# A fifth product of a tile with B goes from VectorE to GpSimd, and the w1/w2 ring gets three places

## The chip, the cores and the metric

The kernel runs on one core of one Trainium2 chip. The metric is the device time of one execution in microseconds (us); less is better. The core has TensorE (PE), VectorE (DVE), ScalarE (ACT), GpSimd (POOL) and SyncE (SP), each with its own queue of instructions in order, and they wait for each other on semaphores.

## The reference

All data are float32. The input is x of 4 sequences of 2048 positions and 256 features. First a Mamba block with a residual, then a gated feed-forward block with a residual, each closed by a LayerNorm:

```
xz = x @ in_proj.T;  xc, z = halves (512 channels each)
u = silu(causal_conv(xc, 4 taps) + bias)
dt_lo, B, C = split(u @ x_proj.T)            # 64, 16, 16
delta = softplus(dt_lo @ dt_proj.T + dt_b);  A = -exp(A_log)
for t:  h = exp(delta_t * A) * h + (delta_t * u_t) * B_t;  y_t = sum_n h * C_t
x = layernorm(x + ((y + u*D) * silu(z)) @ out_proj.T)
g = silu((x @ w1.T)*s1) * ((x @ w2.T)*s2)    # 1024 wide
g = gelu((g @ h1.T)*s_h1);  g = gelu((g @ h2.T)*s_h2)
x = layernorm(x + (g @ w3.T)*s3)
```

The state h has 512 channels x 16 state numbers per sequence.

## The kernel before

There are two stages. The first (`mamba_stage`) goes over 16 tiles of 512 positions, four per sequence: the whole Mamba block, the LayerNorm and the products with w1 and w2, whose results are stored. The second does the wide layers h1, h2 and w3 on TensorE. The change lies in the first stage alone.

A tile's scans. The 512 channels are taken in four chunks c of 128. A chunk has four steps q of four state numbers each, so a tile has 16 steps k = 4c + q. A step has four groups j, each 128 partitions (32 channels x 4 state numbers) by 512 positions. So a tile has 64 groups. For a group ScalarE computes the decay into a PSUM bank (`decay_of`, L916), and VectorE runs one scan (L1284) over decay and db into h.

db, the product (delta*u)*B of a step, is one instruction of 128x2048. For q = 0, 1, 2 it is VectorE's (`times_b`, L1268): TensorE spreads B's rows over the partitions into PSUM (`spread_b`, L632), and VectorE multiplies by du_bc. For q = 3 (QV) it is GpSimd's (`times_b`, L1155), which can't read PSUM: once a tile ScalarE copies the spread rows into b_row in SBUF (`rows_sb`, L865), the same rows for all four chunks. GpSimd also has the products of h with C (`times_c`, L1144), two pieces of 128x1024 a step, and two small products of softplus per chunk (L1163, L1167). TensorE sums these over the state numbers (`fold_step`, L659).

The order is written out by hand. Every engine runs through 64 slots i of a tile; n = i + 20 is the group that VectorE scans in the slot (n from 64 on is the next tile). In a slot with n = 4m GpSimd does, in this order: the first piece of C of step m-1, the product with B of step m+1 if it is its own, and the second piece of step m-1. VectorE does the scan of group n and then its product of step m+1. Softplus of the next tile's chunk 0 has slots 21 to 27, on GpSimd 26 and 27 (n = 46, 47).

Rings. db has two places (DBSTEPS): the product of step k waits until the scans of step k-2 are done, and the first scan of step k waits for the product. h has three places, the last step of a tile takes that of the step two before it; hc has two. There are three banks for decays, which run two slots ahead.

w1 and w2 come in eight chunks m of 256 KB through a ring of W12RING = 4 buffers. `copy_product` on ScalarE issues the load of chunk m + 4 behind the second product of chunk m (products e = 2m, 2m+1, slots AB_PLACES), the last four being the next tile's. For the last tile's products a closing pass (`closing`) runs all 16 in a row.

The LayerNorm of the tile (L952, slot 15), its transposes on TensorE (L687, slots 16 to 21), and the x_proj results (L851, L852, slot 18) lie near the new copy's slot. p_dt is a PSUM bank that the softplus steps and the first transpose share.

Of the kernel before, what the change touches and what calls it, by code (L numbers as in the profile page):

```python
# [36 lines left out]

QV = QN - 1
EPS = 1e-5
EXP_LN = "natural_log_exp_and_others"  # L40
# [58 lines left out]
ROWS_SLOTS = (42, 44, 46, 50, 54)  # L99
ROWS = len(ROWS_SLOTS)  # L100
X_SLOTS = (47, 48, 49, 49, 51, 52, 53, 53)

# [16 lines left out]
AB = len(AB_PLACES)  # L119
ABRING, W12RING = 3, 4  # L120
W12_SLOTS = (2, 30)
# [74 lines left out]
def mamba_stage(nc, sems, flag, xT, x, in_wT, conv_w, conv_b, xp_wT, dt_wT, dt_b, A_log, D_param, out_wT,  # L196
                fold, spread, ident, w1T, w2T, h1T, h2T, w3T, scales, d_rows, du_rows, w12, x1, ab):
    ctx = ExitStack()
    with ctx:
# [38 lines left out]
        x_t = [sb(f"x_t{i}", [P, KM, NT], F32R) for i in range(2)]  # L238
        w12_sb = [sb(f"w12_{i}", [P, 2, KM, P], F32R) for i in range(W12RING)]
        ab_sbuf = [sb(f"ab{i}", [P, NT]) for i in range(ABRING)]  # L240
        res = sb("res", [P, SUB, DM])
# [70 lines left out]

        b_bc = sem("b_bc")
        decay = sem("decay")
        db_dve, db_pool = sem("db_dve"), sem("db_pool")
# [85 lines left out]
        def _(sp):  # L401
# [21 lines left out]
            def copies(t, c):  # L423

                k = c % 2
                sp.wait_ge(delta, t.count(KI, c + 1))
                sp.dma_start(d_rows[k], sp_r[k][:]).then_inc(d_out[k], 16)
                sp.wait_ge(du, t.count(KI, c + 1))
                sp.dma_start(du_rows[k], sp_w[k][:]).then_inc(du_out[k], 16)

                sp.wait_ge(db_dve, t.count(KI * QV, QV * (c - 1) + DVE0))
                sp.sem_inc(waited, 1)
                sp.wait_ge(db_pool, t.count(KI, c - 1 + POOL0))
                sp.sem_inc(waited, 1)
                sp.wait_ge(du_out[k], t.count(32, 16 * (c // 2 + 1)))
                for nn in range(GN):
                    sp.dma_start(du_bc[k][nn * GD:(nn + 1) * GD, :, :],
                                 du_rows[k].rearrange("(j d) t -> d j t", d=GD)).then_inc(du_in[k], 16)

                sp.wait_ge(decay, t.count(NG, GC * (c - 1) + DECAY0))  # L440
                sp.sem_inc(waited, 1)
                sp.wait_ge(d_out[k], t.count(32, 16 * (c // 2 + 1)))
                for nn in range(GN):
                    sp.dma_start(d_bc[k][nn * GD:(nn + 1) * GD, :, :],
                                 d_rows[k].rearrange("(j d) t -> d j t", d=GD)).then_inc(d_in[k], 16)
# [67 lines left out]
            def closing(t):  # L513
                for m in range(KH):
                    if m == 2:

                        sp.wait_ge(decay, t.count(NG, 3 * GC + DECAY0))
                        sp.wait_ge(db_dve, t.count(KI * QV, 3 * QV + DVE0))
                        sp.wait_ge(db_pool, t.count(KI, 3 + POOL0))
                    elif m == 6:  # L520
                        sp.wait_ge(h1_round, H1_PIECES)
                    sp.dma_start(first_abr[m][:], ab[1, 2 * m:2 * m + 2].rearrange("e p t -> p e t"))\
                      .then_inc(first_in[m // (KH // 2)], 16)
# [16 lines left out]
        def _(pe):  # L540
# [98 lines left out]
            def spread_b(t, k):  # L639
                c, q = divmod(k, QN)  # L640
                if k == 0:
                    pe.wait_ge(xd_lo, t.count(1, 1))

                pe.wait_ge(db_dve, t.count(KI * QV, QV * c + q + DVE0))
                spread_rows(p_b, t, q, b_bc)
# [45 lines left out]
            def transposed(t, k, step):  # L691
                dst = bank[XT_PLACES[k][1]]
                if step == 0:
                    if k == 0:
                        pe.wait_ge(ln_out, t.count(SUB, SUB))
                        pe.wait_ge(sp_dve, t.count(2 * KI, 2 * KI) if exists(t) else t.count(2 * KI, 0))
                    elif exists(t.following()):
# [8 lines left out]
            def ffn_product(t, e):  # L706
# [5 lines left out]
                if which == 0:  # L712
                    pe.wait_ge(w12_in[m % W12RING], t.count(16 * KH // W12RING, 16 * (m // W12RING + 1)))
                before = product_before(t, e)
# [65 lines left out]
            def tile(t):  # L780
                nxt = t.following()
                for i in range(NG):
# [5 lines left out]
                    if n % JC == 1:  # L788
                        now, g = at_group(t, n - 1 + 2 * JC)
                        if exists(now) and g // JC % QN < QV:  # L790
                            spread_b(now, g // JC)
# [7 lines left out]
                    for part in OUT_SLOTS.get(i, ()):  # L799
                        if exists(t):  # L800
                            project(t, *part)
                    if exists(t):
                        ffn(t, i)
                    if t is LAST_ROW[-1] and i == FIRST_SLOT:
# [11 lines left out]
        def _(act):  # L816
# [8 lines left out]
            def front(t, i):  # L825
# [28 lines left out]
                elif i - 1 in ROWS_SLOTS:  # L854
                    r = ROWS_SLOTS.index(i - 1)
                    act.wait_ge(rows_mm, t.count(ROWS, r + 1))
                    if r == 1:

                        act.wait_ge(db_pool, t.count(KI, POOL0))
                        dst = b_row[:]  # L860
# [128 lines left out]
            def copy_product(t, e):  # L989
# [8 lines left out]
                elif e % 2 == 1 and exists(t):  # L998
                    load_w12(t.following(), m - KH)

# [81 lines left out]
            def tile(t):  # L1082
                nxt = t.following()
                for i in range(NG):
# [26 lines left out]
                    if exists(nxt.following()):  # L1111
                        early(nxt.following(), i)
                    if exists(t):
                        ffn(t, i)
                    if t is LAST_ROW[-1]:
# [12 lines left out]
        def _(pool):  # L1128
# [19 lines left out]
            def times_b(t, k):  # L1148

                c = k // QN  # L1150
                pool.wait_ge(du_in[c % 2], t.count(2 * COPIES, COPIES * (c // 2 + 1)))
                if c == 0:
                    pool.wait_ge(rows_sb, t.count(ROWS, 2))
                pool.wait_ge(scanned, t.count(NG, JC * (k - DBSTEPS + 1) + SCANNED0))
                pool.tensor_tensor(db[:, k % DBSTEPS], du_bc[c % 2][:],  # L1155
                                   b_row[:].unsqueeze(1).broadcast_to([P, JC, NT]), ALU.mult).then_inc(db_pool, 1)

# [30 lines left out]
            def tile(t):  # L1188
                nxt = t.following()
                for i in range(NG):  # L1190
# [4 lines left out]
                    if n % JC == 0:  # L1195
# [3 lines left out]
                        now, g = at_group(t, n + JC)  # L1199
                        if exists(now) and g // JC % QN == QV:  # L1200
                            times_b(now, g // JC)
# [9 lines left out]
            def round_piece(j):  # L1211

                if j == 0:

                    pool.wait_ge(first_lo, KH)
                    pool.wait_ge(db_dve, LAST_ROW[-1].count(KI * QV, KI * QV + DVE0))
                    pool.wait_ge(folded, LAST_ROW[-1].count(NK, NK + FOLDED0))
# [24 lines left out]
        def _(dve):  # L1242
# [19 lines left out]
            def times_b(t, k):  # L1262
                c, q = divmod(k, QN)
                dve.wait_ge(b_bc, t.count(KI * QV, QV * c + q + 1))
                if q == 0:
# [5 lines left out]
            def scan(t, g):  # L1271
# [3 lines left out]
                if j == 0:  # L1275
                    if q < QV:
                        dve.wait_ge(db_dve, t.count(KI * QV, QV * c + q + 1 + DVE0))
                    else:
                        dve.wait_ge(db_pool, t.count(KI, c + 1 + POOL0))
                    dve.wait_ge(saved, t.count(NK, holder_before(H_SLOT, k) + 1 + SAVED0))  # L1280
# [43 lines left out]
            def closing(t, i):  # L1324
# [6 lines left out]
                elif i == GATE_SLOT + 3:  # L1331
                    for m in range(KH):
                        dve.wait_ge(first_hi, m + 1)
                        if m == 0:

                            dve.wait_ge(decay, t.count(NG, NG + DECAY0))
                            dve.wait_ge(db_pool, t.count(KI, KI + POOL0))
                        dve.tensor_tensor(first_parts[1][:, m, :], first_abr[m][:, 1, :],
# [9 lines left out]
            def tile(t):  # L1348
                nxt = t.following()
                for i in range(NG):  # L1350
# [10 lines left out]
                    if n % JC == 0:  # L1361
                        now, g = at_group(t, n + JC)
                        if exists(now) and g // JC % QN < QV:
                            times_b(now, g // JC)
# [740 lines left out]
```

## Time and profile before

| what | us |
|---|---|
| median of 3 runs | 3012.06 |
| lowest, highest | 3010.54, 3012.91 |
| the profiled execution | 3011.42 |
| its span in the profile | 3009.6 |
| busy in the span: PE, DVE, ACT, POOL | 2720.0, 2297.7, 2033.7, 1704.2 |

The busy times are over both stages. In the profile's slices GpSimd is at 8 or 9 tenths up to slice 24 of 40 and at nothing later, VectorE at 9 up to slice 25 and at 4 later. A timeline merges instructions of a kind that follow each other; x5 is five of them, and the time is that from the first's start to the last's end.

### The profile page before, as it was taken

The numbers are of one execution on the slowest core, as the hardware profiler recorded it, in microseconds if no ns is written. First come the engines' busy times: TensorE is split into PE (matmuls) and PEld (weight loads), VectorE is DVE, ScalarE is ACT, GpSimd is POOL, SyncE is SP. The second block draws the span as 40 slices with busy tenths as digits, with TensorE's granted clock in tenths as the row PEclk, the third lists the DMA queues.
The fourth block names the chain that finished last, engine by engine and source line by source line (L and its number), as shares of the span: only waits on it lengthen the run. The fifth ranks groups of instructions, "written<-read, shape, count | busy, mean of one in ns | idle before, by whom it ended". The sixth has DMA issues, their size and how long they took to land. (4 is left out here: it accounts for less than half of the span.)

```text
span 3009.6 us, 40984 instructions
## 1 busy us (share of the span) xinstructions
PE 2720.0 (90%) x11540; PEld 1619.3 (54%) x11540; DVE 2297.7 (76%) x2650; ACT 2033.7 (68%) x3600; POOL 1704.2 (57%) x839
## 2 busy tenths in 40 slices
PE   5798998998998998998998976999999999999997
PEld 2243443343443443443443432778888888888886
DVE  6999999999999999999999999144445444444452
ACT  3878877878878877877878877465544555555452
POOL 4899999999899989999999998100000000000000
PEclk8899999998999999999999987999999999999999
DMA  8565565565566565565565566632222222222210
GB/s 265 122 188 158 144 190 158 144 193 164 134 193 165 136 192 159 139 196 158 139 192 165 143 186 224 205 101 77 92 70 70 84 91 77 70 79 88 70 42 15
DMA packets 239646, 412.05 MB, mean 137 GB/s; under 512 B 23264, under 2 KB 63456, under 8 KB 239456
## 3 DMA queue, kind: packets, MB, share of 16 engines
q1 hardware_dynamic: 175680, 297.67, 36.6%
q10 hardware_dynamic: 63776, 112.22, 11.4%
q8 instruction: 73, 1.20, 0.2%
q14 instruction: 117, 0.96, 0.1%
HBM read 285.55 MB, written 124.26 MB: 136 GB/s over the span
## 5 line engine op out<-in xcount | busy, mean ns | idle before, releaser
L1284 DVE TENSOR_TENSOR_SCAN h<-bank,state,db 128x512 f32<-128x512 f32 x1024 | 1243.3, 1268 | 18.9 <-ACT bank L916 18.5
L1144 POOL TENSOR_TENSOR hc<-h,c_rows 128x1024 f32<-128x1024 f32 x512 | 1200.3, 2375 | 96.6 <-DVE h L1284 75.0
L916 ACT ACTIVATE bank<-d_bc,a_neg 128x512 f32<-128x512 f32 x1024 | 695.4, 685 | 251.8 <-DVE h L1284 240.6
L1625 ACT ACTIVATE hring<-s_bank,sc 128x512 f32<-128x512 f32 x248 | 170.4, 687 | 488.6 <-PE s_bank L1558 488.3
L1558 PE MATMUL s_bank<-mid,h_r 128*128 128x512 f32 x2048 | 468.7, 390 | 4.6 <-DVEq L1652 4.6
L1268 DVE TENSOR_TENSOR db<-bank,du_bc 128x2048 f32<-128x2048 f32 x192 | 435.7, 2269 | 2.5 <-issue 2.5
L1558 PEld LDWEIGHTS s_bank<-mid,h_r 128*128 128x128 f32 x2048 | 385.5, 188 | 85.6 <-ACTq L1596 5.0
L731 PE MATMUL bank<-x_t,w 128*128 128x512 f32 x1088 | 362.5, 461 | 60.7 <-ACT ab L993 53.9
L659 PE MATMUL bank<-hc,fold_w 128*32 128x512 f32 x2048 | 305.1, 671 | 23.0 <-DVE uz L1308 11.3
L731 PEld LDWEIGHTS bank<-x_t,w 128*128 128x128 f32 x1088 | 203.2, 200 | 216.6 <-ACT ab L993 101.0
L1155 POOL TENSOR_TENSOR db<-du_bc,b_row 128x2048 f32<-128x2048 f32 x64 | 291.4, 4553 | 16.0 <-DVE h L1284 15.9
L585 PE MATMUL bank<-xb,w_conv 128*128 128x512 f32 x512 | 241.9, 611 | 3.6 <-ACT res L927 2.8
L632 PE MATMUL bank<-bc,w_spread 64*128 64x512 f32 x272 | 138.0, 519 | 112.5 <-DVE db L1268 86.0
L1558 PE MATMUL s_bank<-s_end,h_r 128*128 128x512 f32 x1024 | 235.7, 391 | 0.0
L632 PEld LDWEIGHTS bank<-bc,w_spread 64*128 64x128 f32 x272 | 51.7, 196 | 333.6 <-DVE db L1268 172.5
L1683 DVE TENSOR_TENSOR mid<-hring,mid 128x512 fp32r<-128x512 f32 x120 | 81.5, 690 | 177.6 <-ACT mid L1628 177.6
L1558 PEld LDWEIGHTS s_bank<-s_end,h_r 128*128 128x128 f32 x1024 | 191.8, 188 | 41.4
L993 ACT ACTIVATE ab<-bank 128x512 f32<-128x512 f32 x272 | 159.1, 585 | 54.0 <-PE bank L731 47.1
L1558 PE MATMUL s_bank<-first_lo,h_r 128*128 128x512 f32 x448 | 175.4, 391 | 0.0
L1558 PE MATMUL s_bank<-first_hi,h_r 128*128 128x512 f32 x448 | 175.3, 391 | 0.0
L585 PEld LDWEIGHTS bank<-xb,w_conv 128*128 128x128 f32 x512 | 91.3, 190 | 126.7 <-issue 123.3
L1683 DVE TENSOR_TENSOR first_lo<-hring,first_hi 128x512 fp32r<-128x512 f32 x64 | 44.3, 691 | 147.1 <-ACT first_hi L1628 147.1
(147 smaller groups left out, 3721.7 us busy)
## 6 DMA issues: line engine op xcount, KB each, us to landing
ab<-ab ACTq DMA_DIRECT2D x272, 256.0 KB, 3.8
du_bc<-du_rows SPq DMA_DIRECT2D x256, 256.0 KB, 4.7
d_bc<-d_rows SPq DMA_DIRECT2D x256, 256.0 KB, 7.7
s_abr<-ab SPq DMA_DIRECT2D x120, 512.0 KB, 3.7
w<-w ACTq DMA_DIRECT2D x136, 256.0 KB, 3.1
d_rows<-sp_r SPq DMA_DIRECT2D x64, 256.0 KB, 2.0
du_rows<-sp_w SPq DMA_DIRECT2D x64, 256.0 KB, 3.1
x<-res SPq DMA_DIRECT2D x17, 512.0 KB, 8.8
```

Source lines behind the costliest of these rows:

```text
L585: last = pe.matmul(p_mm[j % 2][:], w_conv[:, c, k, :], xb[:, c, k:k + NT], start=k == 0, stop=k == TAPS - 1)
L632: pe.matmul(dst[:], spread_w[:, which, :], bc[t.tt % 2][DTR:P, :], start=True, stop=True).then_inc(done, 1)
L659: last = pe.matmul(p_y[GD * j:GD * j + GD, :], fold_w[:], hc[:, k % HCSTEPS, j, :], start=q == 0, stop=q == QN - 1, tile_position=(0, GD * j))
L731: last = pe.matmul(product_bank(t, e)[:], w12_sb[m % W12RING][:, which, k, :], x_t[j][:, k, :], start=k == 0 and j == 0, stop=k == KM - 1 ...
L916: act.activation(decays[DECAY_BANK[g]][:], d_bc[c % 2][:, j, :], ACT.Exp, scale=a_neg[:, g:g + 1]).then_inc(decay, 1)
L993: act.activation(ab_sbuf[e % ABRING][:], product_bank(t, e)[:], ACT.Copy, scale=-1.0).then_inc(ab_sb, 1)
L1144: pool.tensor_tensor(hc[:, k % HCSTEPS, at:at + HG], h[:, H_SLOT[k], at:at + HG], c_rows[:, q, :].unsqueeze(1).broadcast_to([P, HG, NT]), ...
L1155: pool.tensor_tensor(db[:, k % DBSTEPS], du_bc[c % 2][:], b_row[:].unsqueeze(1).broadcast_to([P, JC, NT]), ALU.mult).then_inc(db_pool, 1)
L1268: dve.tensor_tensor(db[:, k % DBSTEPS], p_b[:].unsqueeze(1).broadcast_to([P, JC, NT]), du_bc[c % 2][:], ALU.mult).then_inc(db_dve, 1)
L1284: dve.tensor_tensor_scan(h[:, H_SLOT[k], j, :], decays[DECAY_BANK[g]][:], db[:, k % DBSTEPS, j, :], state[:, g:g + 1], ALU.mult, ALU.add). ...
L1558: last = pe.matmul(p_h[m % HBANKS][:], hidden_weights(layer, k, m), ins[j][:, k, :], start=k == 0 and j == 0, stop=k == KH - 1 and j == pa ...
L1625: act.activation(hring[c % RING][:], p_h[m % HBANKS][:], ACT.Gelu, scale=sc[:, 2 + layer, m:m + 1]).then_inc(gelu, 1)
```

## The change

QV steps stay with GpSimd, and step 13 (chunk 3, q = 1) joins them. For it a second row tile b_row2 of 128x512 is needed: TensorE spreads B's rows for q = 1 into the bank p_dt in slot 13, and ScalarE copies them in slot 14. b_row2 takes SBUF space that the fourth w1/w2 buffer had, so the ring has three. The waits on counts of products are rewritten for 5 and 11 a tile instead of 4 and 12.

```
+EXTRA_Q, EXTRA_C = 1, 3
+BY_POOL = [k % QN == QV or k == QN * EXTRA_C + EXTRA_Q for k in range(NK)]
+NPOOL = sum(BY_POOL)
+NDVE = NK - NPOOL
+def pool_steps(k):
+    return k // NK * NPOOL + sum(BY_POOL[:k % NK])
+def dve_steps(k):
+    return k - pool_steps(k)
+ROW2_SLOT = 13
-ABRING, W12RING = 3, 4
+ABRING, W12RING = 3, 3
+        b_row2 = sb("b_row2", [P, NT])
...
@@ SP, copies (the same rewriting in closing, and on the other engines)
-                sp.wait_ge(db_dve, t.count(KI * QV, QV * (c - 1) + DVE0))
+                sp.wait_ge(db_dve, t.count(NDVE, dve_steps(QN * (c - 1)) + DVE0))
-                sp.wait_ge(db_pool, t.count(KI, c - 1 + POOL0))
+                sp.wait_ge(db_pool, t.count(NPOOL, pool_steps(QN * (c - 1)) + POOL0))
...
@@ PE, transposed, step 0 of k = 0
-                        pe.wait_ge(sp_dve, t.count(2 * KI, 2 * KI) if exists(t) else t.count(2 * KI, 0))
+                        pe.wait_ge(row2_sb, t.count(1, 1) if exists(t) else t.count(1, 0))
@@ PE, ffn_product
-                    pe.wait_ge(w12_in[m % W12RING], t.count(16 * KH // W12RING, 16 * (m // W12RING + 1)))
+                    pe.wait_ge(w12_in[m % W12RING], t.count(16 * len(range(m % W12RING, KH, W12RING)), 16 * (m // W12RING + 1)))
@@ PE, tile
-                        if exists(now) and g // JC % QN < QV:
+                        if exists(now) and not BY_POOL[g // JC]:
                             spread_b(now, g // JC)
...
                     if exists(t):
+                        if i == ROW2_SLOT:
+                            pe.wait_ge(sp_dve, t.count(2 * KI, 2 * KI))
+                            spread_rows(p_dt, t, EXTRA_Q, row2_mm)
                         ffn(t, i)
@@ ACT, copy_product
-                    load_w12(t.following(), m - KH)
+                    load_w12(t.following(), e // 2 % W12RING)
@@ ACT, tile
                     if exists(t):
+                        if i == ROW2_SLOT + 1:
+                            act.wait_ge(row2_mm, t.count(1, 1))
+                            act.wait_ge(db_pool, t.count(NPOOL, POOL0))
+                            act.activation(b_row2[:], p_dt[:], ACT.Copy).then_inc(row2_sb, 1)
                         ffn(t, i)
@@ POOL, times_b
-                c = k // QN
+                c, q = divmod(k, QN)
+                row = b_row if q == QV else b_row2
                 pool.wait_ge(du_in[c % 2], t.count(2 * COPIES, COPIES * (c // 2 + 1)))
-                if c == 0:
-                    pool.wait_ge(rows_sb, t.count(ROWS, 2))
+                if q == QV:
+                    if c == 0:
+                        pool.wait_ge(rows_sb, t.count(ROWS, 2))
+                else:
+                    pool.wait_ge(row2_sb, t.count(1, 1))
                 pool.wait_ge(scanned, t.count(NG, JC * (k - DBSTEPS + 1) + SCANNED0))
                 pool.tensor_tensor(db[:, k % DBSTEPS], du_bc[c % 2][:],
-                                   b_row[:].unsqueeze(1).broadcast_to([P, JC, NT]), ALU.mult).then_inc(db_pool, 1)
+                                   row[:].unsqueeze(1).broadcast_to([P, JC, NT]), ALU.mult).then_inc(db_pool, 1)
@@ POOL, tile
-                        if exists(now) and g // JC % QN == QV:
+                        if exists(now) and BY_POOL[g // JC]:
                             times_b(now, g // JC)
@@ DVE, scan
-                    if q < QV:
-                        dve.wait_ge(db_dve, t.count(KI * QV, QV * c + q + 1 + DVE0))
+                    if BY_POOL[k]:
+                        dve.wait_ge(db_pool, t.count(NPOOL, pool_steps(k) + 1 + POOL0))
                     else:
-                        dve.wait_ge(db_pool, t.count(KI, c + 1 + POOL0))
+                        dve.wait_ge(db_dve, t.count(NDVE, dve_steps(k) + 1 + DVE0))
@@ DVE, tile
-                        if exists(now) and g // JC % QN < QV:
+                        if exists(now) and not BY_POOL[g // JC]:
                             times_b(now, g // JC)
```

## Rows read from the trace of the kernel before

**Rows 1.** The page's part 1: busy us, share of span, instructions.

```profile
PE 2720.0 (90%) x11540; PEld 1619.3 (54%) x11540; DVE 2297.7 (76%) x2650; ACT 2033.7 (68%) x3600; POOL 1704.2 (57%) x839
```

**Rows 2.** Stretches of one tile each: length, busy (instructions), clock, DMA share, GB/s.

```profile
902.02:1013.75 111.73, 99.08 (x393) 43.05 (x393) 109.93 (x90) 89.83 (x171) 104.02 (x50) 0.95 0.62 166
339.19:451.79 112.60, 100.75 (x396) 43.64 (x395) 109.92 (x90) 89.80 (x171) 104.03 (x50) 0.95 0.61 165
```

**Rows 3.** VectorE's timeline in one tile: start, us, engine, line, operation [idle before].

```profile
367.45 0.69 DVE L1302 TENSOR_TENSOR bc<-bank,bc 32x512 fp32r<-32x512 f32 x1 [1.15 <-ACT bc L852]
...
378.68 0.66 DVE L1295 SCALAR_TENSOR_TENSOR sp_e<-bank,sp_e 128x512 f32<-128x512 f32 x1
...
382.81 2.27 DVE L1268 TENSOR_TENSOR db<-bank,du_bc 128x2048 f32<-128x2048 f32 x1
384.99 4.80 DVE L1284 TENSOR_TENSOR_SCAN h<-bank,state,db 128x512 f32<-128x512 f32 x4
389.70 2.27 DVE L1268 TENSOR_TENSOR db<-bank,du_bc 128x2048 f32<-128x2048 f32 x1
391.88 3.63 DVE L1284 TENSOR_TENSOR_SCAN h<-bank,state,db 128x512 f32<-128x512 f32 x3
...
396.00 5.98 DVE L1284 TENSOR_TENSOR_SCAN h<-bank,state,db 128x512 f32<-128x512 f32 x5
```

**Rows 4.** GpSimd's timeline in the same tile.

```profile
365.35 2.35 POOL L1144 TENSOR_TENSOR hc<-h,c_rows 128x1024 f32<-128x1024 f32 x1 [0.73 <-PE bank L659]
367.66 4.54 POOL L1155 TENSOR_TENSOR db<-du_bc,b_row 128x2048 f32<-128x2048 f32 x1
372.16 7.04 POOL L1144 TENSOR_TENSOR hc<-h,c_rows 128x1024 f32<-128x1024 f32 x3
379.51 1.30 POOL L1163 TENSOR_TENSOR sp_r<-sp_r,sp_e 128x512 f32<-128x512 f32 x1 [0.30 <-DVE sp_e L1295]
380.96 1.27 POOL L1167 TENSOR_TENSOR sp_w<-sp_r,u 128x512 f32<-128x512 f32 x1 [0.16 <-POOL sp_r L1163]
382.19 9.38 POOL L1144 TENSOR_TENSOR hc<-h,c_rows 128x1024 f32<-128x1024 f32 x4
393.24 2.35 POOL L1144 TENSOR_TENSOR hc<-h,c_rows 128x1024 f32<-128x1024 f32 x1 [1.67 <-DVE h L1284]
395.59 4.55 POOL L1155 TENSOR_TENSOR db<-du_bc,b_row 128x2048 f32<-128x2048 f32 x1
```

**Rows 5.** Timelines of GpSimd and VectorE in another tile.

```profile
943.97 9.38 POOL L1144 TENSOR_TENSOR hc<-h,c_rows 128x1024 f32<-128x1024 f32 x4
...
957.72 5.98 DVE L1284 TENSOR_TENSOR_SCAN h<-bank,state,db 128x512 f32<-128x512 f32 x5
```

**Rows 6.** TensorE's timeline in the tile of rows 3.

```profile
361.41 1.88 PE L687 MATMUL bank<-w_id,res 128*128 128x128 f32 x8 [2.24 <-ACT res L952]
363.22 1.94 PE L659 MATMUL bank<-hc,fold_w 128*32 128x512 f32 x8
```

**Rows 7.** Groups by line: count, busy us, mean ns, idle before.

```profile
L865 ACT ACTIVATE c_rows<-bank 128x512 f32<-128x512 f32 x64 | 37.4, 585 | 1.6 <-PE bank L632 0.9
```

**Rows 8.** ScalarE's timeline in the tile of rows 3.

```profile
358.00 1.28 ACT L916 ACTIVATE bank<-d_bc,a_neg 128x512 f32<-128x512 f32 x2
359.22 2.06 ACT L952 ACTIVATE res<-res,a_nb,y 128x256 f32<-128x256 f32 x4
...
366.83 0.59 ACT L852 ACTIVATE bc<-bank 32x512 fp32r<-32x512 f32 x1
```

**Rows 9.** The loads of w1 and w2 (L972), from issue to landing.

```profile
DMA to landing us min/median/max: 2.6/3.1/9.1
```

**Rows 10.** ScalarE's timeline in the closing pass, copies of products 9 and 14.

```profile
1935.65 0.60 ACT L993 ACTIVATE ab<-bank 128x512 f32<-128x512 f32 x1 [0.47 <-ACT ab L993]
...
1941.00 0.60 ACT L993 ACTIVATE ab<-bank 128x512 f32<-128x512 f32 x1 [0.47 <-PE bank L731]
```

**Rows 11.** Timelines of GpSimd and VectorE in the last tile.

```profile
1839.87 9.53 POOL L1144 TENSOR_TENSOR hc<-h,c_rows 128x1024 f32<-128x1024 f32 x4
1843.30 4.80 DVE L1284 TENSOR_TENSOR_SCAN h<-bank,state,db 128x512 f32<-128x512 f32 x4
1854.31 9.51 DVE L1284 TENSOR_TENSOR_SCAN h<-bank,state,db 128x512 f32<-128x512 f32 x8
```

More of the change, by code:

```diff
@@ L313, in mamba_stage @@
         b_bc = sem("b_bc")
+        row2_mm, row2_sb = sem("row2_mm"), sem("row2_sb")
         decay = sem("decay")
@@ L517, in closing @@
                         sp.wait_ge(decay, t.count(NG, 3 * GC + DECAY0))
-                        sp.wait_ge(db_dve, t.count(KI * QV, 3 * QV + DVE0))
-                        sp.wait_ge(db_pool, t.count(KI, 3 + POOL0))
+                        sp.wait_ge(db_dve, t.count(NDVE, dve_steps(3 * QN) + DVE0))
+                        sp.wait_ge(db_pool, t.count(NPOOL, pool_steps(3 * QN) + POOL0))
                     elif m == 6:
@@ L642, in spread_b @@
                     pe.wait_ge(xd_lo, t.count(1, 1))
-                pe.wait_ge(db_dve, t.count(KI * QV, QV * c + q + DVE0))
+                pe.wait_ge(db_dve, t.count(NDVE, dve_steps(k) + DVE0))
                 spread_rows(p_b, t, q, b_bc)
@@ L857, in front @@
                     if r == 1:
-                        act.wait_ge(db_pool, t.count(KI, POOL0))
+                        act.wait_ge(db_pool, t.count(NPOOL, POOL0))
                         dst = b_row[:]
@@ L1113, in tile @@
                     if exists(t):
+                        if i == ROW2_SLOT + 1:
+                            act.wait_ge(row2_mm, t.count(1, 1))
+                            act.wait_ge(db_pool, t.count(NPOOL, POOL0))
+                            act.activation(b_row2[:], p_dt[:], ACT.Copy).then_inc(row2_sb, 1)
                         ffn(t, i)
@@ L1215, in round_piece @@
                     pool.wait_ge(first_lo, KH)
-                    pool.wait_ge(db_dve, LAST_ROW[-1].count(KI * QV, KI * QV + DVE0))
+                    pool.wait_ge(db_dve, LAST_ROW[-1].count(NDVE, NDVE + DVE0))
                     pool.wait_ge(folded, LAST_ROW[-1].count(NK, NK + FOLDED0))
@@ L1263, in times_b @@
                 c, q = divmod(k, QN)
-                dve.wait_ge(b_bc, t.count(KI * QV, QV * c + q + 1))
+                dve.wait_ge(b_bc, t.count(NDVE, dve_steps(k) + 1))
                 if q == 0:
@@ L1336, in closing @@
                             dve.wait_ge(decay, t.count(NG, NG + DECAY0))
-                            dve.wait_ge(db_pool, t.count(KI, KI + POOL0))
+                            dve.wait_ge(db_pool, t.count(NPOOL, NPOOL + POOL0))
                         dve.tensor_tensor(first_parts[1][:, m, :], first_abr[m][:, 1, :],
```

## The prediction

> **What bounds the kernel now.** First the busy line [rows 1]: TensorE has most busy time over the whole span, but the span has two stages. Up to about 1860 us VectorE runs the scans of 16 tiles; after that TensorE alone sets the time with the feed-forward layers, which the change doesn't touch. So I read the first stage by tiles [rows 2]. A tile takes 112.60 us (a few take 111.73), and VectorE is busy 109.9 of them: it is the bound. GpSimd is busy 104.0. It looks as if it had 8.5 us to spare, and one product with B costs 4.5.
>
> That is an average, and the order of the work decides. So next I read the timelines of VectorE and GpSimd over the second half of one tile [rows 3, 4]. The reader is to see that GpSimd runs from 367.66 to 391.57 with under 0.5 us of gaps, and that its idle time (1.67 us before 393.24, 0.73 before 365.35) lies at other places. The rings make slack at one place useless at another: a product for step k may not start before the scans of step k-2 are done (db has two places), and the scans of step k can't start before it has ended.
>
> **Unit prices** from these rows, start to start, since ends overlap starts by some 0.05 to 0.1. A scan: (4.80 - 1.27)/3 = 1.18. A product on VectorE: 384.99 - 382.81 = 2.18. On GpSimd: 372.16 - 367.66 = 4.50. A piece of h times C (two per step): (9.38 - 2.35)/3 = 2.34.
>
> **Part 1, the product leaves VectorE.** It saves 2.18 a tile where nothing else waits: 16 x 2.18 = 34.9 us at most.
>
> **Part 2, it is put into GpSimd's queue** between the first and the second piece of step 11 (slot n = 48). Walk through the tile of [rows 3, 4], with the times of before. GpSimd starts the first piece of step 11 at 382.19, behind the two softplus products of the next tile's chunk 0 (379.51, 380.96). It ends at 384.53. Product 13 starts there and is done at about 384.53 + 4.55 = 389.1; with 0.1 for the semaphore the scans of step 13 start at 389.2. VectorE before started them at 384.99 + 3 x 1.18 = 388.52, and would now be free at 388.52 - 2.18 = 386.34. So it waits 2.8 us: the saving is gone, and step 13 starts 0.66 later than before.
>
> From product 13 to product 15 there are four pieces on GpSimd (second of 11, both of 12, first of 13): 4.50 + 4 x 2.34 = 13.86 from start to start. So product 15 starts at 398.39 (before: 395.59) and ends at 402.9. VectorE needs from the first scan of 13 to the first of 15: 8 scans, one product, one gate, which before took (396.00 + 4 x 1.18) - 388.52 = 12.2. It is at step 15 at 401.4 and must wait until 403.0, another 1.6. Before, step 15 started at 400.7. So step 15 is 2.3 us late. Between the two GpSimd itself doesn't wait: the first piece of 13 needs two scans of 13, done at 389.2 + 1.18 + 2.18 + 1.27 = 393.8, and GpSimd gets there at 396.1.
>
> Is the delay given back later? GpSimd has 1.67 idle ahead of the matching piece of the next tile, which takes up what it is later than VectorE. VectorE has nothing: behind step 15 it is busy without gaps and everything (decays, spreads, DMAs) waits for its scans, so its delay passes into the next tile. The same walk in a tile of the other kind [rows 5]: piece 11 starts at 943.97, product 15 would end at 943.97 + 2.34 + 4.50 + 9.36 + 4.55 = 964.7, step 15 at 964.8 instead of 957.72 + 4.71 = 962.43: +2.4.
>
> **Part 3, the new row of B.** TensorE gets a spread at slot 13 in place of one at n = 45 (count unchanged, some 0.5 us). It waits for the softplus of chunk 3, whose last VectorE step has slot 11, and on TensorE it stands behind the slot's own spread, which waits for VectorE's product of slot 12, so 0 for that wait. Behind it TensorE has room: it waits 2.24 us for ScalarE before the transposes at 361.41 [rows 6]. ScalarE gets a copy of 128x512 from PSUM, 0.585 by the like copy of L865 [rows 7], some 0.5 start to start. It stands behind the decay of slot 14. Its other wait, for GpSimd's last products of the tile before, is long past. Here ScalarE is in a backlog: two decays at 358.00, then at once the four LayerNorm writes at 359.22 [rows 8], which release TensorE's transposes, and behind these the fold of step 7 (363.22 [rows 6]), for which GpSimd waits 0.73 before the first piece of step 9 (365.35) and so starts product 11 later. The same backlog ends in the copy of bc (366.83), for which VectorE waits 1.15 (367.45), and it is VectorE's softplus step (378.68) for which GpSimd waits 0.30 (379.51). All these gaps are zero-slack, so the 0.5 goes in full into the chain up to product 13. The lower bound is 0 (the copy falls into a gap; a gain is excluded, since nothing is taken off ScalarE), the upper 0.6, its whole length. I take 0.5, since every link of the chain shows a wait now. Step 15 is then 2.8 late.
>
> **Part 4, three w1/w2 buffers.** The loads stay eight a tile on the same queue. In the loop the chunk loaded behind product 1 (slot 26) is needed by product 6 (slot 34), some 8 x 112.6/64 = 14 us later; the slowest load landed in 9.1 [rows 9]: 0. In the closing pass the products stand close together; the last load goes out behind the copy of product 9 (1935.65) and its weights are used just ahead of the copy of product 14 (1941.00 [rows 10]), some 4.5 us, against a median of 3.1 and that 9.1. So 0 to 4 us once; I take 0.
>
> **Part 5, the last tile** has no softplus of a next tile before product 13. GpSimd's first piece of step 11 starts at 1839.87 [rows 11] and ends at 1842.2; product 13 is done at 1846.8, and VectorE, which was at step 13 at 1843.30 + 3.54 = 1846.84, starts it at about the same time as before. Product 15 then starts at 1842.2 + 13.86 = 1856.1 and ends at 1860.6; step 15 comes at 1860.7 instead of 1854.31 + 4.71 = 1859.0: 1.7, and 2.2 with part 3. Behind it GpSimd's pieces hold TensorE and through it the closing, so I pass 2.2 on.
>
> **Sum**: 15 x 2.8 + 2.2 = 44.2 us. The profiled execution took 3011.42 (span 3009.6), the median of the runs is 3012.06, so 0.6 more: 3056. The same check from the idle time: 112.6 + 2.8 = 115.4 a tile, of which GpSimd busy 104.0 + 4.6 = 108.6, VectorE 107.7: neither is full, and the tile is longer all the same.
>
> **A rule of the skill.** The scans beside GpSimd's long product (five in 5.98 from 396.00, 1.18 each [rows 3]) take what those beside a shorter piece take (four in 4.80 from 384.99): the two engines don't slow each other. The Trainium skill, "SBUF — State Buffer", Who interferes with whom, says that a VectorE instruction with two SBUF inputs blocks against a GpSimd one that reads SBUF. A scan reads its decay from PSUM and only db as a stream from SBUF, so by that rule as by the row there is no extra; if the state column counted as a second input, each added product would hold VectorE up for its length.
>
> **Rivals.**
> (a) *Faster: the product is hidden.* Product 13 is ready before VectorE has scanned step 12, and product 15 too. Then 16 x 2.18 are saved: 2977. For it: 8.5 us of GpSimd idle a tile. Against: it decides whether product 13 ends by 386.3 in the shown tile, and the queue ahead of it is gapless back to 367.66, so it would have to be 2.8 us shorter. 7 in 100.
> (b) *Only the first wait is paid.* Step 15 isn't later than step 13 is (the four pieces find slack, or VectorE's 2.7 us of other gaps a tile shrink by the delay): 0.66 + 0.5 = 1.2 a tile, 3031. For it: other engines catch up in the stall. Against: those gaps follow VectorE's own scans. 8 in 100.
> (c) *Cascade.* TensorE is held at the folds of steps 11 and 13 by the late pieces, its products for ScalarE come late, and decays fall behind: one more us a tile, about the size of VectorE's one wait for ScalarE in [rows 3] (1.15): 3072. Against: TensorE is busy 100.8 of 112.6 [rows 2], and its gaps are mostly waits for VectorE. 9 in 100.
> (d) *Contention* by the lock: 4.5 more of stalls a tile, 72 us: 3128. 1 in 100.
> (e) *Cancelling*: half of the two waits is absorbed and the copy costs nothing, near 3012. 3 in 100.
>
> **Numbers.** The forecast has 72 in 100. Its own range: 2.3 a tile (copy free) is 3048, 3.2 a tile 3063. The range takes in (b) and (c), since without either it would leave more than 2 in 10 out: 3030 to 3072. A measurement of this kernel tells a change from none at about 0.2%, 6 us. Slower: the forecast, (b), (c), (d), 0.90. Same 0.03. Faster 0.07.
>
> **What would show it.** In the profile after: VectorE idle before the first scan of step 13 by about 2.8 us and of step 15 by about 1.6, both released by GpSimd's db; some 70 us in all of such waits on L1284, which has none now. The tile at about 115.4. GpSimd idle about 7 us a tile. The low-rows wait 0.5 longer. If the tile is under 112 or the db waits under 30 us, the walk is wrong.

## The result: 1.6% slower, as the walk said

The changed kernel takes 3060.85 us (median of 4 runs, 3054.38 to 3062.03) against 3012.48 of the kernel before: ratio 1.0157, 95% interval 1.014 to 1.0175. Predicted were 3056 and a range of 3030 to 3072. The profiled execution took 3062.03, its span is 3060.2; the span before was 3009.6, so the two traces differ by 50.6.

First the page's groups of instructions after, by line (busy us, mean ns, idle before). They answer to VectorE's scans, its products with B, GpSimd's pieces and products, and TensorE's folds.

```profile
L1316 DVE TENSOR_TENSOR_SCAN h<-bank,state,db 128x512 f32<-128x512 f32 x1024 | 1245.7, 1266 | 89.7 <-POOL db L1187 52.7
L1172 POOL TENSOR_TENSOR hc<-h,c_rows 128x1024 f32<-128x1024 f32 x512 | 1200.1, 2375 | 79.2 <-DVE h L1316 41.8
L1300 DVE TENSOR_TENSOR db<-bank,du_bc 128x2048 f32<-128x2048 f32 x176 | 398.8, 2266 | 2.3 <-issue 2.3
L678 PE MATMUL bank<-hc,fold_w 128*32 128x512 f32 x2048 | 305.3, 671 | 87.4 <-POOL hc L1172 78.1
L1187 POOL TENSOR_TENSOR db<-du_bc,b_row 128x2048 f32<-128x2048 f32 x80 | 364.8, 4560 | 12.7 <-DVE h L1316 12.7
```

The counts are those of the change: 80 products on GpSimd, 176 on VectorE, with unchanged durations. What is new is idle time. VectorE stands 89.7 us ahead of its scans (18.9 before), of which the page puts 52.7 to GpSimd's products. TensorE stands 87.4 us ahead of its folds (23.0 before), of which 78.1 are put to GpSimd's pieces. Two stretches of one tile each (length, busy of PE, PEld, DVE, ACT, POOL, clock, DMA) answer to [rows 2]:

```profile
461.17:578.07 116.90, 100.77 (x394) 44.43 (x393) 108.06 (x89) 90.45 (x172) 108.55 (x52) 0.94 0.59 158
578.07:692.60 114.53, 101.88 (x399) 43.73 (x397) 108.04 (x89) 90.09 (x172) 108.53 (x52) 0.96 0.60 161
```

VectorE is 1.9 less busy a tile, GpSimd 4.5 more, neither is full, and the tile is 2 to 4 us longer than the 112.60 of [rows 2]. Nearly all of the 50.6 us arises in the first stage: its last LayerNorm starts at 1953.49, before at 1903.92.

VectorE's timeline after, over the end of a tile (start, us, line, operation [idle before]); it answers to [rows 3]:

```profile
385.31 7.15 DVE L1316 TENSOR_TENSOR_SCAN h<-bank,state,db 128x512 f32<-128x512 f32 x6
395.36 1.28 DVE L1316 TENSOR_TENSOR_SCAN h<-bank,state,db 128x512 f32<-128x512 f32 x1 [2.89 <-POOL db L1187]
396.56 2.27 DVE L1300 TENSOR_TENSOR db<-bank,du_bc 128x2048 f32<-128x2048 f32 x1
398.74 3.62 DVE L1316 TENSOR_TENSOR_SCAN h<-bank,state,db 128x512 f32<-128x512 f32 x3
402.28 0.67 DVE L1340 TENSOR_TENSOR uz<-bank,uz 128x512 f32<-128x512 f32 x1
402.86 4.80 DVE L1316 TENSOR_TENSOR_SCAN h<-bank,state,db 128x512 f32<-128x512 f32 x4
409.16 1.28 DVE L1316 TENSOR_TENSOR_SCAN h<-bank,state,db 128x512 f32<-128x512 f32 x1 [1.50 <-POOL db L1187]
...
441.75 1.28 DVE L1316 TENSOR_TENSOR_SCAN h<-bank,state,db 128x512 f32<-128x512 f32 x1 [0.43 <-ACT bank L939]
443.98 0.70 DVE L1323 SCALAR_TENSOR_TENSOR bank<-sp_w,bank 128x512 f32<-128x512 f32 x1 [0.95 <-ACT bank L912]
```

GpSimd's in the same stretch, against [rows 4]:

```profile
371.39 2.36 POOL L1172 TENSOR_TENSOR hc<-h,c_rows 128x1024 f32<-128x1024 f32 x1 [1.09 <-PE bank L678]
373.72 4.53 POOL L1187 TENSOR_TENSOR db<-du_bc,b_row 128x2048 f32<-128x2048 f32 x1
...
388.25 2.38 POOL L1172 TENSOR_TENSOR hc<-h,c_rows 128x1024 f32<-128x1024 f32 x1
390.60 4.55 POOL L1187 TENSOR_TENSOR db<-du_bc,b_row 128x2048 f32<-128x2048 f32 x1
395.11 9.34 POOL L1172 TENSOR_TENSOR hc<-h,c_rows 128x1024 f32<-128x1024 f32 x4
404.39 4.57 POOL L1187 TENSOR_TENSOR db<-du_bc,b_row 128x2048 f32<-128x2048 f32 x1
```

The reader is to see the chain: product 13 ends at 395.15 and the first scan of step 13 starts 0.2 later; four pieces; product 15 ends at 408.96 and step 15 starts at 409.16. The two waits are 2.89 and 1.50 (predicted 2.8 and 1.6). From product 11 to product 15 GpSimd takes 404.39 - 373.72 = 30.67; before it took 27.93 for the same stretch, of which 1.67 was idle [rows 4].

### The profile page after: what moved, and what is told of

It is laid out like the page before. It is cut to its first block and busy times, and to the rows that moved or that the text cites. A ratio compares the mean times of both kernels' runs of the same rounds, so it can differ in the third digit from the quotient of the medians.

```text
span 3060.2 us, 41091 instructions
## 1 busy us (share of the span) xinstructions
PE 2743.6 (90%) x11540; PEld 1635.1 (53%) x11540; DVE 2269.3 (74%) x2634; ACT 2042.1 (67%) x3616; POOL 1775.3 (58%) x855
## 5 line engine op out<-in xcount | busy, mean ns | idle before, releaser
L1316 DVE TENSOR_TENSOR_SCAN h<-bank,state,db 128x512 f32<-128x512 f32 x1024 | 1245.7, 1266 | 89.7 <-POOL db L1187 52.7
L750 PE MATMUL bank<-x_t,w 128*128 128x512 f32 x1088 | 375.6, 472 | 33.2 <-ACT ab L1016 17.0
L1300 DVE TENSOR_TENSOR db<-bank,du_bc 128x2048 f32<-128x2048 f32 x176 | 398.8, 2266 | 2.3 <-issue 2.3
L678 PE MATMUL bank<-hc,fold_w 128*32 128x512 f32 x2048 | 305.3, 671 | 87.4 <-POOL hc L1172 78.1
L1187 POOL TENSOR_TENSOR db<-du_bc,b_row 128x2048 f32<-128x2048 f32 x80 | 364.8, 4560 | 12.7 <-DVE h L1316 12.7
L750 PEld LDWEIGHTS bank<-x_t,w 128*128 128x128 f32 x1088 | 209.6, 206 | 198.2 <-issue 94.9
L678 PEld LDWEIGHTS bank<-hc,fold_w 128*32 128x32 f32 x2048 | 42.0, 112 | 229.0 <-POOL hc L1172 121.6
```

The costliest lines, as they stand in the source:

```text
L678: last = pe.matmul(p_y[GD * j:GD * j + GD, :], fold_w[:], hc[:, k % HCSTEPS, j, :], start=q == 0, stop=q == QN - 1, tile_position=(0, GD * j))
L750: last = pe.matmul(product_bank(t, e)[:], w12_sb[m % W12RING][:, which, k, :], x_t[j][:, k, :], start=k == 0 and j == 0, stop=k == KM - 1 ...
L1187: pool.tensor_tensor(db[:, k % DBSTEPS], du_bc[c % 2][:], row[:].unsqueeze(1).broadcast_to([P, JC, NT]), ALU.mult).then_inc(db_pool, 1)
L1300: dve.tensor_tensor(db[:, k % DBSTEPS], p_b[:].unsqueeze(1).broadcast_to([P, JC, NT]), du_bc[c % 2][:], ALU.mult).then_inc(db_dve, 1)
L1316: dve.tensor_tensor_scan(h[:, H_SLOT[k], j, :], decays[DECAY_BANK[g]][:], db[:, k % DBSTEPS, j, :], state[:, g:g + 1], ALU.mult, ALU.add). ...
```

## The experiments

Theory Q: GpSimd's queue makes the wait. The products 13 and 15 and what stands between them are late, and the same work at another place would cost otherwise. Its first rivals: W, the shorter w1/w2 ring; R, the new row in a full stretch of ScalarE; and the total work on GpSimd, wherever it stands. All medians are beside runs of the kernel before on the same chip (3011.97 to 3013.91).

**The ring alone** (the kernel before with this, the counts that go with three buffers, and an unused tile in the free space):

```
-ABRING, W12RING = 3, 4
+ABRING, W12RING = 3, 3
```

> The kernel before with only the ring of w1/w2 cut to three places (an unused tile fills the space). Theory Q (the wait is made by GpSimd's queue: product 13, then four pieces, then product 15) expects no change, 3012 +- 3. Rival W (the shorter ring costs, in the loop or in the closing pass) expects 3016 or more, and over 3030 if it carries a large part of the 48 us.

Measured 3014.57, ratio 1.0006 (0.9996 to 1.0016). The ring is no measurable part of it, and rival W falls.

**The row alone** (the kernel after with this; the ring of three stays):

```
-BY_POOL = [k % QN == QV or k == QN * EXTRA_C + EXTRA_Q for k in range(NK)]
+BY_POOL = [k % QN == QV for k in range(NK)]
```

> The kernel after, but step 13's product stays with VectorE; only the spread in slot 13, ScalarE's copy in slot 14 and the ring of three are left (b_row2 is written and not read; TensorE has one spread a tile more than in either kernel). Theory Q with the term of part 3 expects at most 0.5 us a tile, 3016 to 3020. Rival R (the new row in a full stretch of ScalarE is the main cost) expects over 3035.

Measured 3017.31, ratio 1.0011 (1.0002 to 1.0021): 3 us by the ratio, 5 by the medians, and at most 6 by the interval. Rival R falls.

**The row elsewhere**, product 13 still on GpSimd:

```
-ROW2_SLOT = 13
+ROW2_SLOT = 33
...
+                            pe.wait_ge(db_dve, t.count(NDVE, NDVE + DVE0))
+                            spread_rows(p_b, nxt, EXTRA_Q, row2_mm)
...
+                        act.activation(b_row2[:], p_b[:], ACT.Copy).then_inc(row2_sb, 1)
```

> The kernel after, with the spread of the new row moved to slot 33 of the tile before (bank p_b, free there) and the copy to slot 34, away from the LayerNorm; product 13 stays on GpSimd. Theory Q expects the two waits of VectorE for GpSimd's product unchanged in kind, the first 0.5 shorter: about 8 us less than after, 3053. Rival R expects most of the 48 us gone, under 3030.

Measured 3059.11, ratio 1.0161 (1.014 to 1.0182): not told apart from the 1.0157 of after. It was expected some 8 us below after, and it is 2 below, which is within the noise. So I had over-sized the row. Who kept VectorE waiting in the first stage, in this kernel's trace (total us, times, longest):

```profile
DVE h L1316 <- POOL db L1187: 52.5, 24, 2.9
DVE h L1316 <- ACT bank L940: 25.3, 30, 1.9
DVE bank L1323 <- ACT bank L913: 15.5, 32, 1.0
DVE h L1316 <- issue: 11.9, 6, 2.8
DVE bc L1334 <- ACT bc L876: 5.6, 5, 1.2
```

and the same view of after:

```profile
DVE h L1316 <- POOL db L1187: 52.7, 24, 3.0
DVE h L1316 <- ACT bank L939: 20.0, 32, 1.6
DVE bank L1323 <- ACT bank L912: 16.8, 32, 1.0
DVE h L1316 <- issue: 14.8, 7, 2.9
DVE bc L1334 <- ACT bc L875: 11.1, 10, 1.6
```

The wait for bc halves, as it should with the copy gone from there (11.1 to 5.6), but waits for decays take it up (20.0 to 25.3). The "issue" entries are of the size and at the place of the waits for db (one stands at 1895.53, 0.1 after a product's end), so I count them with these: 67.5 in after. One more wait at such a place (step 15 of the last tile, 1.49) is put to ScalarE.

**Half the product:** GpSimd's product 13 over two of the four groups; the other two aren't computed.

```
+                w = JC if q == QV else JC // 2
+                pool.tensor_tensor(db[:, k % DBSTEPS, 0:w], du_bc[c % 2][:, 0:w],
+                                   row[:].unsqueeze(1).broadcast_to([P, w, NT]), ALU.mult).then_inc(db_pool, 1)
```

> The kernel after, with GpSimd's product of step 13 over two of its four groups only (128x1024 instead of 128x2048; the other two groups aren't computed). VectorE has the same work as after; GpSimd has about 2.2 us a tile less ahead of product 15. Theory Q says that the tile follows GpSimd's time one for one as long as VectorE waits: 2.2 us a tile less, 36 us, 3025; the first wait 2.9 falls to about 0.7, the second stays near 1.5. If the cause were the row, the ring or TensorE's folds it would stay at 3055 to 3061.

Measured 3017.29, ratio 1.0013 (1.0002 to 1.0024). VectorE does the same work as in after, and 2.2 us a tile (35 in all) off GpSimd bring 44 us, 8 more than expected. GpSimd's time ahead of product 15 is what the tile waits for. Counted by their place, whatever releaser the profile names, VectorE's waits at steps 13 and 15 fall from 69 to 35 us (2.9 to 0.7 a tile at step 13, 1.5 unchanged at step 15). Its waits for ScalarE fall as well, from 46 to 38 us, and that is about the 9 us beyond the 35. Of the waits at steps 13 and 15 the profile names these as GpSimd's:

```profile
DVE h L1317 <- POOL db L1188: 26.9, 24, 1.5
```

**Other places for the same work.** With the row made in slot 33, any step can be the fifth: `EXTRA_C` 1 is step 5, `EXTRA_C` 2 is step 9.

> As the kernel with the new row made in slot 33, but GpSimd's fifth product is step 5's (second of the second chunk) instead of step 13's. Same work on every engine. Theory Q by the walk in the rows of before: product 5 fits between the pieces of step 3 and is done before VectorE needs it (no wait), then GpSimd's product 7 starts 1.6 later and ends 0.9 after the scans of step 7 were started before; ahead of products 11 and 15 GpSimd's idle time absorbs the rest. 0.9 a tile, 3022 to 3032. A theory in which the amount of work on GpSimd decides, not its place, expects 3055 to 3061 as for step 13.

> The same with step 9's product (second of the third chunk). Theory Q: GpSimd is full between products 7 and 11 (LayerNorm steps and two softplus products lie there), so product 9 is 0.5 late and product 11 2.7 late: 3050 to 3060. A theory in which only the neighbourhood of the tile's last steps is bad expects it near step 5's.

Step 5: 3025.17, ratio 1.0049 (1.0035 to 1.0063), in the walk's range. Step 9: 3069.92, ratio 1.0193 (1.0178 to 1.0209), above it by 10; there too VectorE waits for db (45.9) and, more than I had, for decays (60.8 against 16.5 before, 20.0 in after). The same instructions cost 13, 47 or 58 us by their place alone: the total work on GpSimd isn't the cause. In step 5's trace the wait for a db has moved to product 7, and two waits for decays stand ahead of it:

```profile
444.90 1.28 DVE L1316 TENSOR_TENSOR_SCAN h<-bank,state,db 128x512 f32<-128x512 f32 x1 [1.02 <-ACT bank L940]
...
450.97 2.46 DVE L1316 TENSOR_TENSOR_SCAN h<-bank,state,db 128x512 f32<-128x512 f32 x2 [1.42 <-ACT bank L940]
...
460.36 1.28 DVE L1316 TENSOR_TENSOR_SCAN h<-bank,state,db 128x512 f32<-128x512 f32 x1 [1.63 <-POOL db L1187]
```

In the kernel before, the one wait of this stretch is that for a decay:

```profile
449.25 2.46 DVE L1284 TENSOR_TENSOR_SCAN h<-bank,state,db 128x512 f32<-128x512 f32 x2 [0.96 <-ACT bank L916]
```

The three waits add up to 4.07, 3.1 more than the one. So in this tile VectorE loses the 2.18 it saves and 0.9 more, the 0.9 of the walk. The walk had put all of it at product 7; nearly half stands at decays instead.

**Softplus back to VectorE:** step 5's product on GpSimd, and the two small products of chunk 2 on VectorE.

```
+                elif step == 6:
...
+                    dve.tensor_tensor(sp_r[k][:], sp_r[k][:], sp_e[:], ALU.subtract).then_inc(delta, 1)
+                elif step == 7:
...
+                    dve.tensor_tensor(sp_w[k][:], sp_r[k][:], u_of(t, c), ALU.mult).then_inc(du, 1)
```

> The kernel with step 5's product on GpSimd, and in turn the two softplus products of chunk 2 (128x512 each, slots 60 and 61, right in that stretch) on VectorE. GpSimd has 2.6 less there, VectorE 1.2 more. Theory Q: no wait for GpSimd's products is left there, VectorE's work falls by 2.2 - 1.2 = 1.0 a tile: about 2997, faster than before. Rival L (VectorE instructions with both inputs in SBUF are held up by GpSimd's running ones, which the Trainium skill, SBUF - State Buffer, Who interferes with whom, states; no run has shown it yet here): each of the two waits for one of GpSimd's pieces of 2.3 or product of 4.5, 2 to 5 us a tile lost, 3030 or more.

Measured 3072.08, ratio 1.0208 (1.0195 to 1.0222). Rival L is right. Groups of VectorE in this kernel, 450 to 1000 us:

```profile
L1338 DVE TENSOR_TENSOR sp_r<-sp_r,sp_e 128x512 f32<-128x512 f32 x5 | 20.3, 4055 | 0.0
L1355 DVE TENSOR_TENSOR uz<-bank,uz 128x512 f32<-128x512 f32 x19 | 12.8, 675 | 0.2
L1343 DVE TENSOR_TENSOR sp_w<-sp_r,uz 128x512 f32<-128x512 f32 x5 | 8.2, 1646 | 0.0
```

and the place in its timelines, VectorE and GpSimd:

```profile
452.80 4.05 DVE L1338 TENSOR_TENSOR sp_r<-sp_r,sp_e 128x512 f32<-128x512 f32 x1
457.97 1.65 DVE L1343 TENSOR_TENSOR sp_w<-sp_r,uz 128x512 f32<-128x512 f32 x1
```

```profile
451.74 4.57 POOL L1188 TENSOR_TENSOR db<-du_bc,b_row 128x2048 f32<-128x2048 f32 x1
456.25 5.59 POOL L1173 TENSOR_TENSOR hc<-h,c_rows 128x1024 f32<-128x1024 f32 x2
```

A 128x512 product with one input in PSUM takes 0.675. With both in SBUF it takes 4.05, and ends 0.54 after GpSimd's product that was running (456.31). This is so in all 16 tiles: the instruction starts at different places of GpSimd's product and takes 3.73 to 4.95, but its end stands 0.54 to 0.56 behind the product's. So it has waited for it. GpSimd's two pieces behind take 5.59 instead of 4.7, so GpSimd waits as well. No wait for db is left (GpSimd is early), but the two instructions cost 5.7 a tile instead of the 1.2 I gave them: 16 x 4.5 = 72, and 2997 + 72 = 3069. The Trainium skill ("SBUF — State Buffer", Who interferes with whom) states that a VectorE instruction with two SBUF inputs contends with a GpSimd instruction that reads SBUF. The trace agrees, with the 0.54 behind GpSimd's product.

**Order on GpSimd.** Product 7, or product 15, ahead of both pieces of its slot:

```
-                        if exists(done):
+                        b_first = g // JC == 7        # 15 in the other; in (7, 11) in the third
+                        if exists(done) and not b_first:
                             times_c(done, at // JC, range(1))
...
-                            times_c(done, at // JC, range(1, TURNS))
+                            times_c(done, at // JC, range(0 if b_first else 1, TURNS))
```

> The kernel with step 5's product on GpSimd (new row in slot 33), with one change of order on GpSimd: in the slot of product 7 the product goes ahead of both pieces of step 5. In that kernel's trace VectorE waits 1.6 a tile for product 7, whose start stands behind the first piece of step 5. Theory Q: the wait goes, 1.6 a tile less, 25 us: 2998 to 3003, faster than before. If the wait only moves (to the ring of h, or to TensorE's folds) it stays at 3015 to 3025.

> The kernel after, with one change of order on GpSimd: product 15 goes ahead of both pieces of step 13. All work is the same. Theory Q: three pieces instead of four lie between products 13 and 15; VectorE's second wait (1.5) goes and the first (2.9) stays: 24 us less than after, 3035 to 3040. A theory in which GpSimd's total time per tile sets the pace expects no change, 3055 to 3061.

Theory Q missed both: 3024.98, ratio 1.0037 (1.0024 to 1.0049), and 3065.35, ratio 1.0168 (1.0152 to 1.0183). In the second VectorE still waits at step 15 (1.71 against 1.50 in after), with another releaser:

```profile
394.93 1.28 DVE L1317 TENSOR_TENSOR_SCAN h<-bank,state,db 128x512 f32<-128x512 f32 x1 [2.90 <-POOL db L1187]
...
408.94 1.29 DVE L1317 TENSOR_TENSOR_SCAN h<-bank,state,db 128x512 f32<-128x512 f32 x1 [1.71 <-POOL hc L1172]
```

Step 15 takes step 13's place in the ring of h, so it waits for the first piece of step 13 as well as for product 15. Both must be through GpSimd, in either order. I had left this out. It doesn't speak for total time on GpSimd (step 5 against step 9 does against it), but it says that the stretch before step 15 is full and order can't help. In the first the wait only moved, to product 11 (1.21 a tile). So that one went first too:

> As the kernel with product 7 ahead of the pieces of step 5, and now product 11 also ahead of both pieces of step 9. The trace of the one without has VectorE's wait moved to product 11 (1.2 a tile). Theory Q: product 11 can start when step 9's scans are done, 0.6 before VectorE would wait for its end: the wait goes, 1.2 a tile, 19 us: 3003 to 3008, a little under the kernel before. If GpSimd is full over the whole stretch and the wait moves once more, or ScalarE's decays set the pace there, 3018 to 3026.

Measured 3019.98, ratio 1.0024 (1.0014 to 1.0033). Missed: the waits for GpSimd are down to 5.4 us, the time isn't. VectorE's waits in the first stage:

```profile
DVE h L1317 <- ACT bank L940: 42.6, 50, 1.6
DVE bank L1324 <- ACT bank L913: 13.3, 30, 2.9
DVE bc L1335 <- ACT bc L876: 11.2, 9, 1.3
DVE h L1317 <- POOL db L1187: 5.4, 5, 1.7
```

against the kernel before:

```profile
DVE h L1284 <- ACT bank L916: 16.5, 19, 1.6
DVE bank L1291 <- ACT bank L889: 11.4, 32, 0.9
DVE bc L1302 <- ACT bc L852: 7.9, 7, 1.2
```

The three for ScalarE grew from 35.8 to 67.1 us. That is 31 of the 35 that VectorE saves. With some 7 for GpSimd it comes to 38, 3 more than the saving, where the kernel is 8 us slower; the other 5 stay open. This asked what a product off VectorE is worth at all.

**A product for nothing:** the kernel before, with VectorE's product of one step cut to one of its four groups (three groups aren't computed), nothing added.

```
+                w = JC // 4 if k == 13 else JC        # 5 in the other
+                dve.tensor_tensor(db[:, k % DBSTEPS, 0:w], p_b[:].unsqueeze(1).broadcast_to([P, w, NT]),
+                                  du_bc[c % 2][:, 0:w], ALU.mult).then_inc(db_dve, 1)
```

> The kernel before with VectorE's product of step 13 over one of its four groups (128x512; the other three groups aren't computed) and nothing put anywhere else: 1.6 a tile off VectorE. This prices the rival (a), that the product is hidden. If VectorE alone is the bound, 16 x 1.6 = 26 us less, 2986. If TensorE and ScalarE stand right behind it (theory S, from the kernel with products 7 and 11 first, where the waits for GpSimd are gone and the time isn't), they give back a large part: 2995 to 3010.

> The same cut at step 5, just ahead of the stretch in which VectorE already waits about 1 us for a decay. VectorE alone as the bound: 2986. Theory S expects the gain to be lost in that wait: 3005 to 3012, less gain than at step 13.

At step 13: 2993.11, ratio 0.9937 (0.9924 to 0.9951), 19 us of the 25, just under the 2995 to 3010 of theory S. At step 5: 3010.15, ratio 0.9995 (0.9986 to 1.0004): nothing that can be told from noise, as theory S had it. VectorE's timeline there:

```profile
435.36 0.67 DVE L1269 TENSOR_TENSOR db<-bank,du_bc 128x512 f32<-128x512 f32 x1
435.94 3.63 DVE L1285 TENSOR_TENSOR_SCAN h<-bank,state,db 128x512 f32<-128x512 f32 x3
440.65 1.28 DVE L1285 TENSOR_TENSOR_SCAN h<-bank,state,db 128x512 f32<-128x512 f32 x1 [1.08 <-ACT bank L916]
...
446.68 2.46 DVE L1285 TENSOR_TENSOR_SCAN h<-bank,state,db 128x512 f32<-128x512 f32 x2 [1.37 <-ACT bank L916]
```

The product is 1.6 shorter, and VectorE stands 1.08 us a little later for a decay that it found ready before, and 1.37 where it had waited 0.96 (the line at 449.25 above). So theory S holds at this place: in the stretch of steps 4 and 5 ScalarE stands right behind VectorE. What holds ScalarE there in turn (TensorE's long run of products and projections is my guess) wasn't taken apart. At step 13 VectorE's time counts, but there GpSimd has no room. No version that computes the whole result beat the kernel before.

## Why the prediction was right

- **Part 1**, 2.18 a tile off VectorE: busy 109.9 to 108.05 in the stretches. That is 1.9; I put the rest down to overlap in the busy counts, which no run shows apart. n13_quarter prices it: at step 13 three quarters of the cut come back as time, at step 5 nothing. So 35 us was an upper end, and rival (a)'s 2977 would have been about 2986 by the better of the two rates.
- **Part 2**, the two waits: 2.89 and 1.50 where 2.8 and 1.6 stood; 67.5 us over the tiles where some 70 stood. f4_half shows that they follow GpSimd's time, k5_step5 and k9_step9 that they follow the place. Net of the 2.18 saved, they are 2.2 a tile (predicted 2.3).
- **Part 3**, 0.5 a tile for the row. The links are there: in after GpSimd waits 1.09 for the fold ahead of product 11 (0.73 before [rows 4]) and VectorE 1.57 for bc (1.15 before [rows 3]), so 0.4 each in this tile. But such a wait for bc stands in some tiles only: over the stage it grew from 7.9 to 11.1 us, 0.2 a tile. And the runs give 3 to 5 us for the row alone, not 8, and nothing measurable for moving it. The prediction took every gap of the chain as one without slack, and this term of the sum was over-sized by 3 to 5 us.
- **What I didn't have** is of the size of rival (c), in part: more waits for ScalarE. Over the stage they are 46 us in after and 36 before, 0.7 a tile. The clearest sign lies near the end of chunk 0 of the next tile (0.43 and 0.95 in the timeline above). Before, the second of these is 0.34 in the same tile:

```profile
434.37 0.70 DVE L1291 SCALAR_TENSOR_TENSOR bank<-sp_w,bank 128x512 f32<-128x512 f32 x1 [0.34 <-ACT bank L889]
```

The wait of 0.95 (0.94 to 1.04) stands in 10 of 15 tiles in after and in 2 before. It doesn't come with the ring (2 in f1_ring3) or the row (2 in f2_row_only). It stays when the row is moved (8 in f3_row_late), and becomes rarer when product 13 is halved (4 in f4_half). So these profiles, one of each kernel, speak for the late product. The sum of the waits alone doesn't separate the causes: f2_row_only's profiled execution, the longest of its ten (3022.62), has 45 us of them too. The link that I read from the traces is TensorE: it is held at the folds by the late pieces (9 us of such waits before, 78.1 after, 6 in f2_row_only, 53 in f4_half), and its work for ScalarE comes late. No run isolates this link. These waits differ from tile to tile: the stretch 461.17 to 578.07 takes 2.4 more than the next one (116.90 against 114.53), 1.4 of it for a wait for bc that the next one lacks and 1.0 for longer waits for decays and gates.
- **Two errors nearly cancel.** Predicted 115.4 a tile, measured 115.4 as the mean of the first 15 tiles from LayerNorm to LayerNorm (112.3 before). The mean of before is below the 112.6 that I started from, so the growth is 3.1 and not 2.8. It is made up of 2.2 from the queue and 0.7 from waits for ScalarE, the row's share among them; the last 0.2 is of the size of the two overlaps of 0.1 that the new waits undo. That the forecast lies within 5 us of the measured time, with the row too large and the waits for ScalarE left out, is in part luck.
- **Part 4**: 0, as f1_ring3 has it (1.0006, 0.9996 to 1.0016).
- **Rival (b)** and its reason, that VectorE's later gaps shrink, fell: they grew.

## What to carry to other kernels

An engine's idle share over a period says nothing about a single place: walk the queue of the engine that takes the work between the two rings that tie it to the engine that gives it, and add up what stands between. Price the gain alone first, by cutting the work with nothing put in its place. Of the two steps tried here it is 19 us at one and 0 at the other, and the step where it is worth something is the one where the receiver is full. A wait removed by reordering is worth nothing while a second condition (here the place of h) is fulfilled by the same queue.

## What I had not expected of the hardware

In k5_sp_dve a VectorE instruction of 128x512 with both inputs in SBUF took 4.05 us on the mean beside GpSimd's products, against 0.675 with one input in PSUM; in every tile it ended 0.54 to 0.56 after GpSimd's. All VectorE work of the tiles in the kernel before reads one stream from PSUM and at most one from SBUF (a scan has its state column besides), and its scans keep 1.27 in after too, beside GpSimd at 108.5 of 115 us busy. No run gives a scan two streams from SBUF, so what that would cost isn't shown.
